# Low halves of q and k in one GpSimd instruction, three products of halves for the scores, and a new order of all stages

## The reference

```python
x = x + 0.5 * ffn(layernorm(x))
x = x + attention(layernorm(x))
x = x + 0.5 * ffn(layernorm(x))
```

```python
q = apply_rotary(rmsnorm(q), cos, sin) / sqrt(16);  k = apply_rotary(rmsnorm(k), cos, sin)
scores = where(causal, einsum('bhqd,bhkd->bhqk', q, k), -inf)    # 16 score matrices of 2048 x 2048 per batch
attn = softmax(scores);  attn = attn[:, :, 0] - lam * attn[:, :, 1]
out = layernorm(einsum('bhqk,bhkd->bhqd', attn, v)) * (1 - lambda_init)
out = reshape(out) @ Wproj.T
```

## Time and profile before

| | before |
|---|---|
| time, median of 3 runs | 2256.57 us (2249.22 to 2260.17) |
| the profiled execution: span, which is its time | 2257.2 us |
| instructions | 39699 |
| mean granted TensorE clock | 0.962 |
| busy: TensorE, VectorE, ScalarE, GpSimd | 84%, 74%, 76%, 64% |
| DMA transposes into `k_stack` and `q_stack` | 64 each, 3.3 us to landing |

### The profile page before, as it was taken

One profiled execution on the slowest core, in us unless ns is written; L12 is line 12 of the kernel. 1 busy time (PEld: TensorE's weight loads), 2 busy tenths in 40 slices (PEclk: granted clock), 3 DMA queues, 4 the chain that ended last, 5 costly groups with the idle time before them and its releaser, 6 DMA issues. The chain is left out here.

```text
span 2257.2 us, 39699 instructions
## 1 busy us (share of the span) xinstructions
PE 1906.5 (84%) x13634; PEld 776.0 (34%) x13634; DVE 1677.2 (74%) x3657; ACT 1724.0 (76%) x2598; POOL 1438.6 (64%) x1490
## 2 busy tenths in 40 slices
PE   2577889989989888999989888998998899988845
PEld 1233333333423333343333332343332433432312
DVE  8898988778837897878856897878864978834324
ACT  3446888878887887878888888887888799788842
POOL 3778886767735787766845786667763868723213
PEclk9789999999999999999999999999999999999977
DMA  4134444235212444233412334233231434211102
GB/s 110 27 64 85 72 76 76 50 62 89 42 45 38 71 71 90 59 54 76 75 45 38 73 67 88 45 75 61 52 63 40 81 63 86 52 39 20 35 10 45
DMA packets 477494, 136.19 MB, mean 60 GB/s; under 512 B 458222, under 2 KB 477038, under 8 KB 477294
## 3 DMA queue, kind: packets, MB, share of 16 engines
q1 hardware_dynamic: 477294, 133.65, 31.6%
HBM read 11.96 MB, written 8.39 MB: 9 GB/s over the span
## 5 line engine op out<-in xcount | busy, mean ns | idle before, releaser
L1243 ACT ACTIVATE probs<-psum_s 128x1024 f32<-128x1024 f32 (+3 forms) x1280 | 1072.9, 902 | 109.8 <-PE psum_s L1553 97.9
L1571 PE MATMUL psum_o<-probs,v_sb 128*32 128x512 f32 (+3 forms) x5120 | 581.8, 542 | 27.6 <-POOL probs L1152 14.7
L1514 PE MATMUL shared<-w_gu_T,xT 128*128 128x480 f16 (+1 forms) x2304 | 510.1, 369 | 84.6 <-DMA xT<-x 49.2
L1553 PE MATMUL psum_s<-q_stack,k_stack 64*128 64x512 f16 (+3 forms) x2560 | 390.8, 353 | 101.2 <-ACT probs L1243 91.6
L1514 PEld LDWEIGHTS shared<-w_gu_T,xT 128*128 128x128 f16 x2304 | 212.4, 99 | 371.6 <-issue 102.1
L1527 PE MATMUL shared<-w_down_T,hT 128*128 128x256 f16 x2176 | 272.7, 282 | 36.1 <-DMA hT<-h 16.4
L1166 ACT ACTIVATE hq<-shared,tanh_scale 128x240 f32<-128x240 f32 (+1 forms) x384 | 172.2, 458 | 133.1 <-PE shared L1514 128.2
L1152 POOL TENSOR_SCALAR_AFFINE_SELECT probs<-probs 128x512 f32<-128x512 f32 x256 | 181.3, 715 | 141.3 <-ACT probs L1243 140.0
L1553 PEld LDWEIGHTS psum_s<-q_stack,k_stack 64*128 64x128 f16 x2560 | 94.9, 93 | 508.3 <-ACT probs L1243 409.9
L1120 POOL TENSOR_TENSOR hq<-grid,qscale 128x704 f32<-128x704 f32 x128 | 182.6, 1428 | 112.6 <-DVE grid L1367 112.6
L1083 POOL TENSOR_TENSOR hq<-hq,rscale 128x704 f32<-128x704 f32 x128 | 186.1, 1455 | 104.0 <-DVE rscale L1277 103.8
(11 more groups left out here) (133 smaller groups left out, 2372.8 us busy)
## 6 DMA issues: line engine op xcount, KB each, us to landing
xb<-L_attn_x SPq DMA_DIRECT2D x16, 512.0 KB, 4.1
out<-xb SPq DMA_DIRECT2D x16, 512.0 KB, 2.9
xT<-x SPq DMA_TRANSPOSE x128, 3.1
hT<-h SPq DMA_TRANSPOSE x128, 3.5
k_stack<-st_k SPq DMA_TRANSPOSE x64, 3.3
q_stack<-st_q SPq DMA_TRANSPOSE x64, 3.3
k_stack<-L_ffn_w_down SPq DMA_DIRECT2D x1, 704.0 KB, 4.2
k_stack<-L_ffn_w_gate SPq DMA_DIRECT2D x1, 480.0 KB, 6.0
```

What stands on the lines that cost most here:

```text
L1243: nc.scalar.activation(probs[:, s % 3, 2 * u:2 * u + 2, q0:CHUNK], psum_s[u][:, :, q0:CHUNK], ACT.Exp, scale=HD ** -0.5 / QK_SCALE ** 2).t ...
L1514: last = nc.tensor.matmul(bank(e)[:, 0:2 * (hi - lo)], xs[:, x, t % 2, k, :], w_gu_T[:, w, k, 2 * lo:2 * hi], start=n == 0, stop=n == len( ...
L1553: last = nc.tensor.matmul(psum_s[u][:, j, q0:CHUNK], k_stack[half, at, h, kt % NTC * P:(kt % NTC + 1) * P], q_stack[half, c % 2, h, q0:CHU ...
L1571: last = nc.tensor.matmul(psum_o[at:at + VD, q0:CHUNK], v_sb[:, kt // NTC % SLOTS * NTC + kt % NTC, 2 * g + u, :], probs[:, s % 3, 2 * u + ...
```

## The change

The four-slot stacks now hold q as (high, high, low, zero) and k as (low, high, high, zero), so three products of halves are summed in the place of four: low times low is left out. `st_q` and `st_k` become one tile `st`, and the low halves of q and k of one tile are written by one instruction, which waits for both high halves. `lo_ready` counts one per tile. The fourth slots are set to zero once, in the setup block.

```diff
-        st_q = sb("st_q", [P, ST, 2 * NH, 4, HD], F16)
-        st_k = sb("st_k", [P, ST, 2 * NH, 4, HD], F16)
+        st = sb("st", [P, ST, 2, 2 * NH, 4, HD], F16)
...
+                    nc.gpsimd.memset(st[:, :, :, :, 3, :], 0.0).then_inc(fills_done, 1)
...
-                            sp.wait_ge(lo_ready, 2 * t + 2)
-                            for st, to in ((st_k, k_stack[:, c % SLOTS, :, i * P:(i + 1) * P]),
-                                           (st_q, q_stack[:, c % 2, :, i * P:(i + 1) * P])):
-                                sp.dma_start_transpose(to, st[:, t % ST].rearrange("p a s d -> p (a s d)"))\
+                            sp.wait_ge(hi_ready, 2 * t + 2)
+                            sp.wait_ge(lo_ready, t + 1)
+                            for j, to in ((1, k_stack[:, c % SLOTS, :, i * P:(i + 1) * P]),
+                                          (0, q_stack[:, c % 2, :, i * P:(i + 1) * P])):
+                                sp.dma_start_transpose(to, st[:, t % ST, j].rearrange("p a s d -> p (a s d)"))\
...
-                            for j, (stage, hi, lo) in enumerate(((st_q, slice(0, 2), slice(2, 4)),
-                                                              (st_k, slice(0, 4, 2), slice(1, 4, 2)))):
-                                pool.wait_ge(hi_ready, 2 * t + j + 1)
-                                st = stage[:, t % ST]
-                                src = roped[:, t % NTC, j * C:(j + 1) * C].rearrange("p (h d) -> p h d", d=HD)
-                                nc.gpsimd.tensor_tensor(st[:, :, lo, :],
-                                                        src.unsqueeze(2).broadcast_to([P, 2 * NH, 2, HD]),
-                                                        st[:, :, hi, :], ALU.subtract).then_inc(lo_ready, 1)
+                            pool.wait_ge(hi_ready, 2 * t + 2)
+                            of = st[:, t % ST].rearrange("p j a s d -> p (j a s d)")
+                            n = 2 * NH * 4 * HD
+
+                            def parts(first, step):
+                                return bass.AP(of.tensor, of.offset + first, [of.ap[0], [step, 2], [4 * HD, 2 * NH], [1, HD]])
+                            src = roped[:, t % NTC, :].rearrange("p (j h d) -> p j h d", j=2, d=HD)
+                            nc.gpsimd.tensor_tensor(parts(2 * HD, n - 2 * HD), src, parts(HD, n), ALU.subtract)\
+                                .then_inc(lo_ready, 1)
...
-                            for i, (stage, sl) in enumerate(((st_q, slice(0, 2)), (st_k, slice(0, 4, 2)))):
-                                st = stage[:, t % ST]
+                            for i, sl in enumerate((slice(0, 2), slice(1, 3))):
...
-                                pe.wait_ge(masked, d + 1)
+                                pe.wait_ge(masked, MASK["mask", s] + 1)
```

```diff
-DUE = dict(lead=12, spans=(21, 703, 35, 11832, ...), ..., shift=(...), nudge=dict(...))
+DUE = {
+    "exp0": (83997, 82887, 213431, 149029, 246037, 74985, 193292, 292653, 585327, ...),
+    "mask0": (...), ...
+}
+HOLD = {}
...
-    def add(self, name, engine, weight, due, needs=(), takes=(), frees=(), lands=0.0):
-        weight = COST.get(name[0], weight)
+    def add(self, name, engine, at, needs=(), takes=(), frees=(), lands=0, weight=None):
+        family, c, i, n = at
+        first, last = DUE[family][2 * c:2 * c + 2]
...
-        self.stages[name] = (engine, weight, due + self.nudge.get(name[0], 0),
+        self.stages[name] = (engine, weight, first + (last - first) * i // n,
...
-                    if best is None or (round(start, 6), place[name]) < best[:2]:
+                    key = start - HOLD.get(name[0], 0), place[name]
+                    if best is None or key < best[0]:
```

More of the change, by code:

```diff
@@ L54 @@
 XB = XC * NTC
[L56 to L69, removed]
@@ L175, in order @@
         place = {name: i for i, name in enumerate(sorted(self.stages, key=lambda n: self.stages[n][2]))}
-        met = {name: 0.0 for name in self.stages if not missing[name]}
+        met = {name: 0 for name in self.stages if not missing[name]}
         def ready(name):
@@ L246, in order @@
         self.end = end
+        self.left = left
         return out
@@ L276, in quantise, with fill, of_pair, of_tile @@
-    def quantise(kind, key, due, needs, takes, frees, times):
-        quant, divide, square, grid, points, dequant, high, low, lands = times
+    def fill(name, at, needs, takes=(), frees=()):
+        add(name, "tensor", at, needs, [("bank", name), *takes], frees)
+    def of_pair(kind, pas, p):
+        return kind + str(pas), 2 * p // NTC, p % 2, 1
+    def of_tile(kind, pas, t):
+        return kind + str(pas), t // NTC, t % NTC, NTC - 1
+    def halved(pas, p, made):
+        u = ("x", pas, p)
+        add(("high_x", *u), "scalar", of_pair("high_x", pas, p), [made], [(rings_of(pas)[1], (pas, p))])
+        add(("low_x", *u), "gpsimd", of_pair("low_x", pas, p), [("high_x", *u)], [], [(rings_of(pas)[0], (pas, p))])
+        add(("turn_x", *u), "sync", of_pair("turn_x", pas, p), [("low_x", *u)], [(rings_of(pas)[2], (pas, p))],
+            [(rings_of(pas)[1], (pas, p))], lands=TURNED_X)
@@ L279, in quantise @@
+    def quantise(kind, key, needs, takes, frees):
         own, half, turned = (("xu", "x16", "xT16") if kind == "x" else ("hu", "h16", "hT16"))
         u = (kind, *key)
[L281 to L282 removed]
+        at = lambda stage: (of_pair if kind == "x" else of_tile)(stage, *key)
+        if kind == "x":
             norm, q = ("norm_a", *u), ("scale_x", *u)
[L284 to L287 removed]
@@ L296, in quantise @@
-        add(("high_" + kind, *u), "scalar", high, due + .6, [("dequant_" + kind, *u)], [(half, key)])
-        add(("low_" + kind, *u), "gpsimd", low, due + .7, [("high_" + kind, *u)], [], [(own, key)])
-        add(("turn_" + kind, *u), "sync", .2, due + .8, [("low_" + kind, *u)], [(turned, key)], [(half, key)],
-            lands=lands)
-    def mlp(pas, tiles, due, pace, stats):
+        add(("dequant_" + kind, *u), "gpsimd", at("dequant_" + kind), [("points_" + kind, *u)], [], [place] if kind == "h" else [])
@@ L302, in mlp @@
+        add(("high_" + kind, *u), "scalar", at("high_" + kind), [("dequant_" + kind, *u)], [(half, key)])
+        add(("low_" + kind, *u), "gpsimd", at("low_" + kind), [("high_" + kind, *u)], [], [(own, key)])
+        add(("turn_" + kind, *u), "sync", at("turn_" + kind), [("low_" + kind, *u)], [(turned, key)], [(half, key)],
+            lands=TURNED_X if kind == "x" else TURNED_H)
+    def mlp(pas, tiles, stats):
         for i in range(0, NTC, 2):
-            d = due + pace * i
             pair = (pas, tiles[i] // 2)
-            quantise("x", pair, d, [("rstd", *stats)], [("xu", pair)], [("stats", stats)] if i else [],
-                     (2.3, 1.1, .7, .75, .75, 1.1, .65, 1.35, 3.3))
+            quantise("x", pair, [("rstd", *stats)], [("xu", pair)], [("stats", stats)] if i else [])
@@ L307, in mlp @@
             for t in tiles[i:i + 2]:
                 key = (pas, t)
-                dt = d + 6 + pace * (t % 2)
                 for part in range(len(PARTS)):
                     h = ("hidden", pas, t, part)
-                    d1 = dt + 2 * part
-                    fill(h, 1.3, d1, [("turn_x", "x", *pair), ("hidden", pas, t, part - 1) if part else
-                                      ("hidden", pas, t - 1, len(PARTS) - 1) if t % 2 else None], [("hu", key)],
+                    at = lambda stage: (stage + str(pas), t // NTC, t % NTC * 3 + part, 3 * NTC - 1)
@@ L330, in whole_plan @@
-    due = DUE
-    chunks = range(BATCHES * NCH)
-    at = [0.0, due["lead"]]
-    for c in chunks:
-        at.append(at[-1] + due["spans"][c])
-    for _ in range(4):
-        at.append(at[-1] + due["tail"])
-    def span(x):
-        if x < 0:
-            return x * due["lead"]
-        n = int(x)
-        return at[n] + (x - n) * (at[n + 1] - at[n])
+                fill(dn, of_tile("down", *key), [("turn_h", "h", *key)], [], [("hT16", key)])
+                add(("add_down", pas, t), "vector", of_tile("add_down", *key), [dn], [], [("bank", dn)])
```

291 lines of the change are left out of this document (137 added, 154 removed), and 68 rows, old and new, of the table DUE.

## The result

| | before | after |
|---|---|---|
| median | 2255.15 us (4 runs) | 2242.09 us (2239.18 to 2243.43, 4 runs) |
| ratio after / before | | 0.994, 95% interval 0.9921 to 0.9959 |
| span of the profiled execution | 2257.2 us | 2241.4 us |

The change makes the kernel 0.6% faster, just beyond the 0.5% that the prediction took as the bound to no change. The forecast of 2215 us missed by 27 us, and the rival "only the low halves pay" (2247) came nearest. A run's time is some 2 us more than its span (2243.43 against 2241.4 us for the profiled execution after), so the span before of 2257.2 us belongs to an execution somewhat slower than the median: the two spans lie 15.8 us apart, the medians 13.1.

A forecast was written before the change was run, and what follows sets the result against it. No engine was full; in the mixed stage TensorE and ScalarE waited for each other in turn, a matter of order. From 2257.2 us, 10 for low halves and 32 for the refitted order came off: 2215 us, range 2165 to 2262.

The forecast's parts named there:

- only the low halves pay: Rival for the whole kernel: the refit brings nothing and 10 us from the low halves remain, 2247 us; chance 0.18.
- part 4: Refitted order of all queues: removes a sixth of TensorE's 175.8 us mixed-stage idle time, 32 us with the chain starts.
- The last of the prediction's own signs of being wrong: Profile after: an unchanged idle total would mean that only the low halves' gain, Part 1, is left.
- Part 1: Low halves of q and k on GpSimd: one instruction of 1.26 us per tile instead of two saves 10 us.
- Upper end 20: Low halves later in the chain that ended last: at most 20 us gained, as another chain is close behind.
- Part 2: VectorE's scaling of q and k beside GpSimd: less port contention, counted as 0 us, bounds 0 and 10.
- Part 3: Edits with no price: k's copies, scores products, transposes, zero fill and masks counted by place; 0 us.
- Late masks: Rival: diagonal tiles' masks on GpSimd come late, mask waits double for +42 us, 2289 us; chance 0.12.
- the merged instruction cost as two: Rival on GpSimd: at 2.52 us the merged low halves win nothing, 2225 us with the refit, 2257 without; chance 0.04.
- a rule on tiling modes: TensorE: changing tiling mode drains it; fewer, longer runs save the 0.32 us issue waits before values products, earlier starts add some.

The follow-up runs named there:

- e10: The changed kernel run once more, beside e11 on the same chip: 2241.18 us, 0.9947 of the kernel before.
- e11: The kernel of e1 run once more, beside e10 on the same chip: 2239.92 us, 0.9935 of the kernel before.
- e9: e1's kernel with fixed queues, made from before's order by moving single stages, judged by the planner's plain clock: 2180.4 us, 0.9683 of before.
- e12: e9's order searched further, each move judged by the mean of four replays with stages drawn out by chance: 2160.11 us, 0.9577 of before.
- e3: e1 with low-half cost 1.16 instead of 2.28 in the planner's table, due times as before, queues laid out anew: 2334.28 us, 1.0358 of before.
- e1: The kernel before, stage order untouched, with only the merged low halves and the zero slot: 2238.21 us, 0.9928 of before.
- e4: e1 with low halves made for only one head in sixteen: 2235.68 us, 0.9921 of before.
- e6: e1 with an extra first instruction covering half the heads, so low halves take 1.96 us per tile: 2250.24 us, 0.9974 of before.
- e13: As e12, with chance draws a third as long: 2164.78 us, 0.9605 of before.

## Why the prediction was wrong

**The step that failed is part 4,** the refitted order, at 32 us ("a sixth of 175.8 us"). e10 against e11 shows no gain: the ratios put it 3 us slower, within the noise; the start is 6 us earlier, and the stretch of attention 7 us longer. The fraction was chosen from the size of the idle time and the count of numbers in the table. Neither says how much of it *this* table removes: 175.8 us were idle before, 174.7 after in the same window. That the idle time could be won is right (e9, e12). That 3104 due times could address the pieces "one by one" is not borne out, since in this planner one changed number can act on all that follows (e3). The last of the prediction's own signs of being wrong is what the profile shows: an idle total that hardly changes. Why this refitted order gains nothing on the chip stays open.

**Part 1** was too small, and its mechanism holds only in part. It gave 10 us; e1 and e11 measured 16 and 15 by their ratios. "Upper end 20" held, and so did its price for the merged instruction, 1.26 us (mean 1.24, median 1.158). The 4 to 5 us that it put at the start did not show in e1 and e11: there the first exponential came no earlier than 0.7 us before that of before. What the merge won came from the stretch of attention, and some 2 us from the tail. A fixed share of the low halves on the path, as part 1 reckoned, does not fit e4 either, where another 58 us less of GpSimd's work won next to nothing.

**Part 2** counted 0 for VectorE (bounds 0 and 10). VectorE's busy time fell by 15.9 us in e1 with the same order, 7.6 of them on the scaling of q and k (62.2 to 54.6 us). This agrees with the Trainium skill's rule (SBUF — State Buffer, "Who interferes with whom") that VectorE with two SBUF inputs and GpSimd share a read port. What it is worth in time was not measured apart from the rest of the merge; e4 and e6 say that the time does not follow VectorE's busy time.

**Part 3** held: no row of the high halves, the transposes or the scores products changed by more than a few ns, and the zero fill took 1.0 us in the setup (956 ns after). TensorE's busy total, which was to stay within 10 us, fell by 11.9.

**The rivals.** "Only the low halves pay" is what happened, but that its 2247 us came within 5 us is in part luck: the 13 us are 16 from the merge less some 3 lost by the refit (within the noise), where it had 10 and 0. And the two do not simply add: in the order of before the merge pays 16, in the new order about 30, and the new order costs 19 us when the halves are long. "Late masks" fell: 41.4 us in 82 waits after, 41.7 in 85 before. The masks' place was not the thing to fear; nor did the merged instruction cost as two. The measured 2242 us lies in the stated range, 2165 to 2262, but the forecast gain of 42 us was three times the measured 13.

**Where the prediction weighed a rule on tiling modes.** Values products' weight loads stood on "issue" for 146.1 us before and 167.3 after in the same window. In whole runs, e1 and then e12 (us, times, longest):

```profile
PEld psum_o L1572 <- issue: 166.6, 527, 0.8
PEld psum_s L1554 <- issue: 93.3, 290, 1.4
```

```profile
PEld psum_o L1923 <- issue: 157.1, 555, 0.7
PEld psum_s L1905 <- issue: 138.5, 332, 3.7
```

e12 has more of these waits than e1, 295.6 us against 259.9 of both kinds, and takes 78 us less: so these waits do not explain which of the two orders is faster. The Trainium skill's sentence (TensorEngine Tiling (Array Packing), "Key Properties") that a mode switch has to drain the array names no price, and no run here measures one by itself.

## What to carry to other kernels

Read the two halves of a change apart before adding them: here an edit worth 16 us in one order was worth about 30 in another and 34 in a third. An order that comes out of a greedy planner is not a smooth function of its costs or due times, so refitting those may win back little more than what the new cost upset; moving single stages in fixed queues, judged with durations that vary, won 3.5% on top of the same kernel. And idle time in a profile says what there is to win at most; it is no estimate of what a particular new order takes of it.

## What was not expected

- Freed work on an engine that seemed to bound nothing still paid: GpSimd was 64% busy, and 82 us less of its work gave 16 us; the next 58 us less (e4) gave nothing that can be told from zero.
- The same instructions ran from 2160 to 2334 us by the order of the engines' queues alone (e12, e1, e3).
- The planner's plain clock gave e9 98 us over e1's order, and the chip gave 57. It gave the changed kernel's order 14 us and the chip none, and it ranked e9, e13 and e12 as 2060, 2058 and 2068 where the chip had 2180, 2165 and 2160. The drawn clock ranked the three as the chip did (2170, 2142, 2126). These three orders are in line with tolerance to longer durations as the reason, and are no proof of it; whether it also explains why the changed kernel's order gained nothing was not tested.
